# A gated delta-rule attention layer with a mixture-of-experts layer: the next batch's first stage inside the steps of the batch before, a Relu on ACT, a substitution begun from the negated block

## The reference

```python
def _L0_attn_ref(x, ...):           # H, D = 8, 128; called on _layernorm(x)
    q = short_conv(x @ Wq.T, wq_conv)   # causal, 4 taps per channel, then silu; k and v likewise
    q = scale ** 2 * _rmsn(q, EPS_QK)
    k = scale * _rmsn(k, EPS_QK)
    a_logits = (x @ Wfa.T @ Wfb.T).reshape(B, T, H, D)
    g = -jnp.exp(A_log)[None, None, :, None] * jax.nn.softplus(a_logits + dt_bias)
    beta = jax.nn.sigmoid(x @ Wb.T)

    def step(S, inputs):
        q_t, k_t, v_t, g_t, b_t = inputs
        S = S * jnp.exp(g_t)[..., None]
        kv = jnp.einsum('bhd,bhdv->bhv', k_t, S)
        delta = b_t[..., None] * (v_t - kv)
        S = S + k_t[..., None] * delta[:, :, None, :]
        o = jnp.einsum('bhd,bhdv->bhv', q_t, S)
        return (S, o)
    ...
    gate = (x @ Wga.T @ Wgb.T).reshape(B, T, H, D)
    out = _rmsn(out, EPS_NORM) * o_norm_w * jax.nn.sigmoid(gate)
    return out.reshape(B, T, H * D) @ Wo.T

x = x + _L0_attn_ref(_layernorm(x), ...)
x = x + _L0_ffn_ref(_layernorm(x), ...)   # 8 experts of 128, the best 2 per token, and a shared one
```

## Time and profile before

| | us |
|---|---|
| median of three runs | 5540.53 |
| the profiled execution | 5522.0 |
| its span, first to last instruction | 5520.3 |
| mean granted clock of TensorE | 0.957 |
| attention part, from the first `level(0)` of step 1 to the last | 105.43 to 4613.82 |

### The profile page before, as it was taken

How to read it: one execution, slowest core, us unless ns; L and a number is a source line. 1 busy time by engine, 2 the same in 40 slices (tenths; PEclk the granted TensorE clock), 3 DMA queues, 4 the chain that set the end, 5 groups by cost and what they waited for, 6 DMA issues and landing times.

```text
span 5520.3 us, 115265 instructions
## 1 busy us (share of the span) xinstructions
PE 5037.7 (91%) x30720; PEld 4050.5 (73%) x30720; DVE 4053.8 (73%) x9025; ACT 3239.1 (59%) x6960; POOL 2928.3 (53%) x6466
## 2 busy tenths in 40 slices
PE   3999999999999999999999999999999998999999
PEld 2778787778787778777777777777777787555555
DVE  3778787878787878878787777778787885455555
ACT  2666666667666766666666666666666664111111
POOL 2666666666566666666666666666666664000000
PEclk9999999999999999999999999999999998999999
DMA  2111111111111111111111111111111110000000
GB/s 86 34 34 34 29 34 33 34 35 34 31 34 33 34 33 34 35 34 35 30 33 32 34 34 35 34 35 30 33 33 35 32 34 20 34 9 11 11 11 12
DMA packets 214216, 173.70 MB, mean 31 GB/s; under 512 B 146432, under 2 KB 164096, under 8 KB 213376
## 3 DMA queue, kind: packets, MB, share of 16 engines
q1 hardware_dynamic: 213504, 165.49, 10.3%
HBM read 119.03 MB, written 46.40 MB: 30 GB/s over the span
## 4 chain that ended last, share of the span: by engine, by line
PE 58%; issue 20%; POOL 14%; DVE 5%; POOLq 1%; ACT 1%; DVEq 0%; DMA 0%; SPq 0%; ACTq 0%
PE bank L1290 11%; PE bank L1499 9%; PE bank L1203 8%; POOL mul L394 5%; PE bank L1509 4%; PE bank L1312 4%; POOL rm L398 4%; PE bank L1258 4%; DVE kq L822 3%; POOL tot L411 3%; PE bank L1271 2%; PE bank L1338 2%; PE bank L1217 2%; POOL kl L376 1%; PE bank L1179 1%
## 5 line engine op out<-in xcount | busy, mean ns | idle before, releaser
L376 POOL TENSOR_TENSOR kl<-kl,tot 128x256 f32<-128x256 f32 x768 | 501.0, 652 | 1219.2 <-PE bank L1290 1041.4
L1290 PE MATMUL bank<-kq,kl 128*128 128x128 f32 x6144 | 920.5, 296 | 235.5 <-DVE kq L822 219.9
L1290 PEld LDWEIGHTS bank<-kq,kl 128*128 128x128 f32 x6144 | 796.1, 202 | 300.1 <-issue 250.4
L1203 PE MATMUL bank<-xT,par 128*128 128x512 f32 x1536 | 781.1, 605 | 0.8 <-ACT gaT L524 0.8
L822 DVE TENSOR_TENSOR kq<-kq,tot 128x512 f32<-128x512 f32 x768 | 717.4, 934 | 0.0
L394 POOL TENSOR_TENSOR mul<-pm,rm 32x15 f32<-32x15 f32 (+7 forms) x1920 | 602.8, 314 | 133.2 <-issue 35.0
L398 POOL TENSOR_TENSOR rm<-rm,mul 32x15 f32<-32x15 f32 (+7 forms) x1920 | 589.9, 307 | 151.0
L806 DVE COPY_PREDICATED lx<-mask,bank 128x256 f32<-128x256 uint32 x512 | 297.2, 581 | 269.3 <-PE bank L1290 268.8
L832 DVE COPY_PREDICATED AT<-mask,bank 128x256 f32<-128x256 uint32 x896 | 466.9, 521 | 0.0
L356 POOL TENSOR_TENSOR rstd<-rstd,minus_half 128x4 f32<-128x4 f32 x32 | 32.2, 1007 | 739.7 <-DVE rstd L770 738.1
L1312 PE MATMUL bank<-T,lx 128*128 128x64 f32 x3072 | 400.0, 274 | 5.3 <-issue 0.6
(11 more groups left out here) (171 smaller groups left out, 12957.1 us busy)
## 6 DMA issues: line engine op xcount, KB each, us to landing
par<-params_dram SPq DMA_DIRECT2D x128, 519.0 KB, 3.4
blocks_out<-lx SPq DMA_DIRECT2D x128, 256.0 KB, 2.0
lx<-blocks_in SPq DMA_DIRECT2D x128, 256.0 KB, 2.7
xall<-x_dram SPq DMA_DIRECT2D x16, 512.0 KB, 3.8
pm<-blocks_out SPq DMA_DIRECT2D x512, 8.0 KB
blocks_in<-rm SPq DMA_DIRECT2D x512, 8.0 KB
out_dram<-xall SPq DMA_DIRECT2D x16, 512.0 KB, 2.9
lx<-ffn_dram SPq DMA_DIRECT2D x1, 3456.0 KB, 10.8
```

Of the source, the lines that this page charges most:

```text
L376: pool.tensor_tensor(halves(kl[:, :], w)[:, :, 0, :], src, totr.broadcast_to([P, SEQ // (2 * w), w]), ALU.mult).then_inc(s["kl_ready"], 1)
L1203: ins = pe.matmul(bank[t][:, :], par[p][:, at:at + P], chunk(xT, kt, SEQ), start=kt == 0, stop=kt == KT - 1)
L1290: ins = pe.matmul(dst[:, :, n], chunk(left, n), right[:, :, n, :, 1, :], start=True, stop=True)
```

## The change

`supersteps` is cut one step earlier: five steps of batch 0, then a loop body of steps 5 to 7 of batch b - 1, the (now empty) stage, and steps 0 to 4 of batch b. The moments are formed in step h = 5 and `xn` in step h = 6, both on DVE after `qk_evict(6)` and before `residual_stream(1)`; POOL's power comes after `inverse_norms`. The rest of the first stage runs on PE in step h = 7 between `turn_k` and `project_out(0)`, all through bank `b_q`, on ACT between `gate` and `turned_k`; beta on DVE stays behind the last step. The max with 0 becomes ACT's Relu between the Ln tables' load and `tap0(2)`. `identities` and `eliminate(0)` become `first_columns`: unit block minus the transposed block, at the place of `eliminate(0)`; the later eliminations leave out the diagonal column.

```diff
-            batch_stage(0)
-            steps(0, range(HEADS - 2))
+            batch_stage(0, True)
+            steps(0, range(HEADS - 3))
             with eng.Fori(1, BATCH) as b:
-                steps(b - 1, range(HEADS - 2, HEADS), b)
-                batch_stage(b)
-                steps(b, range(HEADS - 2))
-            steps(BATCH - 1, range(HEADS - 2, HEADS))
+                steps(b - 1, range(HEADS - 3, HEADS), b)
+                batch_stage(b, False)
+                steps(b, range(HEADS - 3))
+            steps(BATCH - 1, range(HEADS - 3, HEADS))
...
-                def identities(iv):
+                def first_columns(iv):
                     after(pool, s["v_out"], 16 * NCH * iv)
-                    pool.tensor_tensor(rm[:, :], eye16[:, :], eye16[:, :], ALU.mult).then_inc(s["sub_step"], 1)
+                    pool.wait_ge(s["low_in"], 16 * NCH * (iv + 1))
+                    square = [t[:, :].rearrange("p (a b) -> p a b", b=BLK) for t in (rm, eye16, pm)]
+                    pool.tensor_tensor(square[0], square[1], square[2].rearrange("p a b -> p b a"), ALU.subtract
+                                       ).then_inc(s["sub_step"], 1)
...
-                    n, m = BLK - 1 - j, j + 1
-                    prod = mul16[:, 0:n * m].rearrange("p (i c) -> p i c", c=m)
+                    n = BLK - 1 - j
+                    prod = mul16[:, 0:n * j].rearrange("p (i c) -> p i c", c=j)
...
@@ POOL's list
                     kl_update(1)
                     kl_update(2)
-                    identities(iB)
...
-                    eliminate(iB, 0)
+                    first_columns(iB)
                     eliminate(iB, 1)
...
-                next_batch()
...
                 if A:
                     inverse_norms()
+                next_rstd()
                 if B:
                     eliminate(iB, 9)
...
@@ ACT
+                def softplus_max():
+                    act.wait_ge(s["f_mm"], i + 1)
+                    after(act, s["t2_done"], i)
+                    act.activation(m_sb[:, :], b_q[:, :], ACT.Relu, bias=par[p][:, DT:DT + 1]).then_inc(s["f_read"], 1)
...
                 if A:
                     softplus_exp()
+                    softplus_max()
                     tap0(2, "v_mm")
                     softplus_ln()
...
                     silu(2)
                     gate()
+                if N:
+                    turned_x(nb, 0)
+                    turned_x(nb, 1)
+                    fa_evict(nb)
+                    ga_evict(nb)
+                    beta_exp(nb)
                 if B:
                     turned_k()
...
@@ DVE
                     conv(1, 3)
-                    softplus_max()
...
                 if C:
                     outputs()
-                next_batch()
...
                     qk_evict(6)
+                next_moments()
+                next_scale()
                 if C:
                     residual_stream(1)
...
@@ PE
+            def turn_next_x(bn, t):
                 pe.wait_ge(s["xn_ok"], bn + 1)
+                after(pe, s["v_mm"], HEADS * bn)
+                if t:
+                    pe.wait_ge(s["xt_ev"], KT * bn + t)
+                else:
+                    after(pe, s["f_read"], HEADS * bn)
+                for n in range(NCH):
+                    ins = pe.transpose(chunk(b_q, n), xn[:, n * HID + t * P:n * HID + (t + 1) * P], ident[:, :])
+                ins.then_inc(s["xnT_mm"], 1)
+
+            def next_fa(bn):
                 pe.wait_ge(s["xt_ev"], KT * (bn + 1))
+                for t in range(KT):
+                    ins = pe.matmul(b_q[:, :], chunk(wfa_sb, t), chunk(xT, t, SEQ), start=t == 0, stop=t == KT - 1)
+                ins.then_inc(s["fa_mm"], 1)
...
@@ PE, project(0, 0)
-                        pe.wait_ge(s["ga_ev"], bt + 1)
+                        pe.wait_ge(s["be_ev"], bt + 1)
...
@@ PE, project_out(0)
                             pe.wait_ge(s["f_read"], i + 1)
+                        if N:
+                            pe.wait_ge(s["be_ev"], nb + 1)
...
@@ PE, the list
                     turn_k()
+                if N:
+                    turn_next_x(nb, 0)
+                    turn_next_x(nb, 1)
+                    next_fa(nb)
+                    next_ga(nb)
+                    next_beta(nb)
                 if C:
                     project_out(0)
```

More of the change, by code:

```diff
@@ L296, in step @@
                     next_params()
-            supersteps(sp, lambda bn: None, step)
+            supersteps(sp, lambda bn, first: None, step)
             sp.wait_ge(s["x_mm"], HIGH * NHEAD)
@@ L440, in inverse_norms, with next_rstd @@
                     pool.tensor_tensor(rinv[p][:, :], tk[p][:, 4:8], plus_half[:, :], ALU.pow).then_inc(s["rinv_done"], 1)
-                def next_batch():
-                    if nb is not None and p == 0:
+                def next_rstd():
+                    if nb is not None and h == HEADS - 3:
                         rstd_of("bn_var", "bn_rs", nb)
@@ L487, in step @@
                     eliminate(iB, 4)
-                next_batch()
-                if B:
                     eliminate(iB, 5)
@@ L502, in _ @@
             rstd_of("bn_var", "bn_rs", 0)
-            supersteps(pool, lambda bn: None, step)
+            supersteps(pool, lambda bn, first: None, step)
             rstd_of("f_var", "f_rs", 0)
@@ L512, in _, with turned_x, beta_exp, fa_evict @@
             act.wait_ge(s["w_in"], 16 * 5)
[L514 to L517, removed]
+            def turned_x(bn, t):
+                act.wait_ge(s["xnT_mm"], KT * bn + t + 1)
+                act.activation(chunk(xT, t, SEQ), b_q[:, :], ACT.Copy).then_inc(s["xt_ev"], 1)
+            def beta_exp(bn):
                 act.wait_ge(s["be_mm"], bn + 1)
                 after(act, s["beta_ok"], bn)
-                act.activation(bexp[:, :], b_s[:, 0:NCH * HEADS], ACT.Exp, scale=-1.0).then_inc(s["be_ev"], 1)
+                act.activation(bexp[:, :], b_q[:, 0:NCH * HEADS], ACT.Exp, scale=-1.0).then_inc(s["be_ev"], 1)
+            def fa_evict(bn):
                 act.wait_ge(s["fa_mm"], bn + 1)
-                act.activation(faT[:, :], b_v[:, :], ACT.Copy).then_inc(s["fa_ev"], 1)
+                act.activation(faT[:, :], b_q[:, :], ACT.Copy).then_inc(s["fa_ev"], 1)
+            def ga_evict(bn):
                 act.wait_ge(s["ga_mm"], bn + 1)
-                act.activation(gaT[:, :], b_x[:, :], ACT.Copy).then_inc(s["ga_ev"], 1)
+                act.activation(gaT[:, :], b_q[:, :], ACT.Copy).then_inc(s["ga_ev"], 1)
+            def batch_stage(bn, first):
+                if first:
+                    turned_x(bn, 0)
+                    turned_x(bn, 1)
+                    fa_evict(bn)
+                    ga_evict(bn)
+                    beta_exp(bn)
             def step(i, h, p, bt, bc, A, B, D, C, nb):
@@ L530, in step @@
                 hc = (h - LAG) % HEADS
+                N = nb is not None and h == HEADS - 1
                 def tap0(t, mm):
@@ L781, in ln_scale, with batch_stage @@
                 ins.then_inc(s[done], 1)
-            def batch_stage(bn):
+            def batch_stage(bn, first):
                 dve.wait_ge(s["be_ev"], bn + 1)
@@ L906, in scales @@
                                       ).then_inc(s["sc_done"], 1)
[L908 to L913, removed]
                 def softplus_one():
@@ new lines, in next_fa, with next_ga @@
+            def next_fa(bn):
+                pe.wait_ge(s["xt_ev"], KT * (bn + 1))
+                for t in range(KT):
+                    ins = pe.matmul(b_q[:, :], chunk(wfa_sb, t), chunk(xT, t, SEQ), start=t == 0, stop=t == KT - 1)
+                ins.then_inc(s["fa_mm"], 1)
+            def next_ga(bn):
+                pe.wait_ge(s["fa_ev"], bn + 1)
+                after(pe, s["g_mm"], HEADS * bn)
+                for t in range(KT):
+                    ins = pe.matmul(b_q[:, :], chunk(wga_sb, t), chunk(xT, t, SEQ), start=t == 0, stop=t == KT - 1)
+                ins.then_inc(s["ga_mm"], 1)
@@ L1174, in batch_stage @@
                 ins.then_inc(s["be_mm"], 1)
[L1175 to L1178, removed]
-                        ins = pe.matmul(dst[:, :], chunk(w, t), chunk(xT, t, SEQ), start=t == 0, stop=t == KT - 1)
-                    ins.then_inc(s[done], 1)
+            def batch_stage(bn, first):
+                if first:
+                    turn_next_x(bn, 0)
+                    turn_next_x(bn, 1)
+                    next_fa(bn)
+                    next_ga(bn)
+                    next_beta(bn)
```

32 lines of the change are left out of this document (13 added, 19 removed).

## The result

The changed kernel takes 5359.0 us (median of four runs, 5349.9 to 5371.0), beside 5539.0 for the kernel before. The profiled execution took 5361.0 us with a span of 5359.2.

A forecast was written before the change was run, and what follows sets the result against it. PE, busy 91% of the span, was taken as the bound, losing time at a gap and the low clock behind it. -137 - 103 + 79 + 27 = -134 us gave 5406 us; own range 5365 to 5455, 5512 with (a) and (b).

The forecast's parts named there:

- the gap: PE's wait at `level(3)` for `kq_update(2)` shrinks: 1.07 us a step gained, 137 us over 128 steps; bounds 0.5 and 1.37.
- the slow stretches: Low-clock stretches of PE in 75 plain steps vanish: 1.37 us each, 103 us gained; bounds 0 and 128.
- counted at nothing: POOL's shorter elimination chain saves less than 1 us a step, but PE waits only 5.9 us there: no gain entered.
- Two edits make this together: Freeing `kq_update(2)` needs both the Relu on ACT and `identities` removed; without `identities` alone, `softplus_low` would still start first.
- The stage: First stage ahead of `project_out(0)`, all through bank `b_q`: 5.2 us lost a batch, 79 us; bounds 3.7 and 7.
- moments and scale: Moments, power and scale one step earlier and later in the step: 1.8 us lost a batch, 27 us.
- I add 1.5 us for slow stretches: Allowance for PE's idle times in the moved stage, raising its 13.0 us delay of `project_out(0)` to 14.5.
- part 1: Relu on ACT and the unit block gone: forecast gains of 137 us and, from slow stretches, 103 us.
- (a): Rival: the gap closes but slow stretches stay, at other places; 5509 us, chance 0.12.
- (b): Rival: ACT's queue behind the Relu loses 0.45 us more; 5464 us, or 5490 with some slow stretches; chance 0.10.
- (c): Rival: `softplus_low` still wins against `kq_update(2)`, so the stall stays; 5646 us, or 5678 with 0.25 more a step; chance 0.09.
- (d): Rival: Relu needs its own table, two 1.28 us loads a step on ACT; 5838 us, chance 0.03.

The follow-up runs named there:

- e3: Kernel before with the Relu on ACT and `first_columns`, the first stage left where it was: 5210.7 us, ratio 0.9425.
- e2: Kernel before with `first_columns` alone, the max with 0 still on DVE: 5412.2 us, ratio 0.9788.
- e1: Kernel before with the Relu on ACT alone, the unit block still written: 5226.6 us, ratio 0.9454.
- e11: e3 with a useless ACT copy of 496 columns added to the Relu: 5290.3 us, ratio 0.9576.
- e5: Kernel before with four unread 128x128 products on PE between `solve(2)` and `level(3)`: 5394.7 us, ratio 0.9759.
- e4: Changed kernel with the Relu and `first_columns` both undone, so the first stage moved alone: 5635.3 us, ratio 1.0184 to the kernel before.
- e8: Changed kernel with moments, power and scale back in the middle of steps 6 and 7: 5333.0 us, ratio 0.9644 to the kernel before.
- e7: e3 with ACT's Relu behind `w_evict(2)` instead of ahead of `tap0(2)`: 5394.4 us, ratio 0.9754 to the kernel before.
- e6: Kernel before with one unread ACT copy of 496 columns ahead of `tap0(2)`, the max with 0 still on DVE: 5232.0 us, ratio 0.9457.

## Why the prediction was wrong

The direction was as forecast, and so was the mechanism, but for the part of the unit block; the sizes were not. Three steps of the sum failed: the gap (137 us forecast, 183 measured), the slow stretches (103 and 139) and the moved stage with its moments (106 and 148). Both sides of the sum were too small, and the errors partly cancelled: 240 us of gain were forecast and 322 measured (e3), 106 of cost forecast and 148 measured (e3 against the changed kernel). That the total came out only 46 us off is luck.

The range failed too. It is said to come "from the bounds of its terms", but these bounds, taken together, give 5540.5 - 175 - 128 + 56 = 5293 at one end and 5540.5 - 64 + 105 + 53 = 5634 at the other. 5365 to 5455 is far narrower, and nothing in the working says why.

**The gap, 1.07 us a step.** "I take 1.07, which is read off this step" was mis-sized; it measured 1.43 (183 us instead of 137), above even the upper bound of 1.37, since that bound held only what `kq_update(2)` could give back. Counted from `level(0)`, `level(1)` of the plain step starts at 5.27, where it was at 5.41, so 0.14 us were gained before the place I looked at. That is POOL's chain, which I "counted at nothing" on the 5.9 us that PE waits for it: with the columns alone (e2) `level(1)` has the new place, with the Relu alone (e1) the old one. The pair e1 and e3 prices the whole edit: 16 us, 0.13 a step, of which a part may come from `kq_update(2)`, 0.69 instead of 0.84. At `state_update(2)` the pair of timelines differs by 14.81 - 13.49 = 1.32, so 1.18 there. I had allowed 0.14 us from the end of `w_evict(2)` to its start, and it was 0.05. The last 0.1 comes behind it; `kq_update(3)` takes 0.68 instead of 0.89, being no longer beside `softplus_high`, but that this is the cause was not tried by itself. That `w_evict(2)` is late next was right (e11).

**The slow stretches, 75 x 1.37 = 103.** The cause was right (e5), the number was low: 475 - 151 = 324 us at the low clock are some 95 stretches of 3.4 us, and they cost 139 us, 1.46 for each stretch instead of 1.37. Giving one stretch a batch to the stage and one to the back edge was a guess. In e3, with the gap closed, the step with the stage has one in about half of the batches, the step behind the back edge in 9 of 14, and the plain steps have none.

**"Two edits make this together"** was wrong. With the Relu alone (e1) the unit block makes the DVE instruction 0.15 us longer and no more. What decides is whether POOL's next instruction is ready when the first one ends.

**The stage, 79 us, and moments and scale, 27 us.** On the old steps 106 was right (103, e4). On the new ones it is 148. e8 gives 26 us to moments and scale, so the stage took 122 and not 79. The chain was read off well: 13.0 us forecast from `project_out(0)` to `project_out(0)`, 13.7 from the first transposes, the slow Wfa product in it. What failed is the term "I add 1.5 us for slow stretches", against a stage today that has one in it: once part 1 has taken the gap away, the old stage has one in about half of the batches (39.34 us at 1.00, 41.05 at 0.96), and the new one has two in most and up to five (0.93 and 0.83), three on average. The step with the stage went from a mean of 40.4 us in e3 to 48.5, which is 8.0 and not 5.2. e4's mean clock, 0.955, is that of before; between e3 and the changed kernel it falls from 0.987 to 0.976, 135 to 257 us at the low clock. At e5's price (139 / 324) these 122 us are some 50 of the 148. The other 98 hold the 26 of e8; the rest was not taken apart.

**The rivals.** (a), the stretches stay elsewhere: no, except in the new stage and in some steps behind the back edge. (b), ACT holds the gain: it took nothing of what was forecast, but e11 shows that ACT's queue has no time left there. (c), the stall stays: e7 and e2 show this case, `softplus_low` first by 0.10 to 0.15 us and 5394 and 5412 with the old stage, so the order of the two starts did decide; after the change the starts are 2039.13 and 2039.62, as read off. (d), table loads: none came; there are still 128 to a line.

By the Trainium skill (ScalarE: Activation LUTs, Rules for kernel authors), relu belongs on VectorE, with a gain that it gives for bf16. Here, in fp32 out of PSUM, the Relu took 0.69 us on ACT and 0.73 on DVE. e7 beside e2 prices taking it off DVE at 18 us, hardly clear of the two intervals, while where it stands in ACT's queue is worth ten times that (e3 beside e7). The other rule of the Trainium skill (SBUF - State Buffer, Who interferes with whom), that whoever issues first gets the shared pair of ports for the whole instruction, agrees with the order seen in e2 and in the changed kernel. In the earlier trace rows it would have let DVE, which had started 0.25 us before POOL's second instruction, go ahead of it; the trace shows the reverse.

## What to carry to other kernels

Compare the longest and the median duration of the same instruction. One that took three times its usual time on DVE beside POOL's instructions was a wait that DVE's idle times didn't show, and here it was cured by one instruction of 0.7 us on ACT, ahead of what POOL's instruction waits for. Then look at the granted clock behind each gap on PE, since a gap of 1.7 us cost another 1.1 us a step in clock. And run each part of a change alone: here one part gained 322 us, the other lost 148, and together they looked like one good change.

## What was not expected of the hardware

Useless work made the kernel faster, twice: one ACT instruction a step (e6, 302 us) and 1.1 us of products a step on PE (e5, 139 us). A DVE instruction that is already waiting can be overtaken by POOL's next one if that follows without a break: in the earlier trace rows it waited through two, in e6 through the rest of one. And POOL's subtraction with a transposed read takes 0.85 us, where the unit block's product of the same number of elements took 0.60; which of the two differences costs it, no run tells.
